# A graph network's gather: a ring of 32 row slots in eight groups in place of 8 slots, and a streamed scale row

## The reference

```python
def gcn_conv(x, W, b, src, dst, n_nodes):      # called twice
    deg  = segment_sum(1, dst) + 1             # with a self loop for every node
    dinv = rsqrt(deg)
    xw   = x @ W
    msg  = xw[src] * (dinv[src] * dinv[dst])
    return segment_sum(msg, dst) + b
out = relu(batch_norm(gcn_conv(layernorm(x), W1, b1, ...)))
out = batch_norm(gcn_conv(out, W2, b2, ...))
x = x + relu(out + layernorm(x))
x = x + moe(layernorm(x))
```

## Time and profile before

| | us |
|---|---|
| the three runs | 7022.28, 7011.63, 6996.64 |
| their median | 7011.63 |
| the profiled execution, span from first to last instruction | 7009.1 |
| aggregation of layer 1, from first to last gather | 295.3 to 2767.7 |
| aggregation of layer 2, from first to last gather | 2908.8 to 5390.0 |

### The profile page before, as it was taken

One profiled execution on the slowest core, in us unless ns is written; L12 is line 12 of the kernel. 1 busy time (PEld: TensorE's weight loads), 2 busy tenths in 40 slices (PEclk: granted clock), 3 DMA queues, 4 the chain that ended last, 5 costly groups with the idle time before them and its releaser, 6 DMA issues. The chain is left out here.

```text
span 7009.1 us, 91724 instructions
## 1 busy us (share of the span) xinstructions
PE 3014.7 (43%) x24826; PEld 1994.5 (28%) x24827; DVE 1748.0 (25%) x6367; ACT 840.1 (12%) x1732; POOL 3732.7 (53%) x3810
## 2 busy tenths in 40 slices
PE   3333333333333334433333333333333443676675
PEld 3222222222222222322222222222222332444443
DVE  9611111111111112511111111111112543222221
ACT  5400000000000000500000000000001542222221
POOL 0266666666666665466666666666664343333333
PEclk5555555555555555555555555555555656888887
DMA  3754444444444443544444444444444343333332
GB/s 90 236 158 133 130 132 133 132 132 132 134 131 132 132 133 109 163 132 134 131 131 132 134 132 133 130 133 130 132 131 114 118 129 106 55 54 53 52 54 45
DMA packets 359556, 847.33 MB, mean 121 GB/s; under 512 B 70751, under 2 KB 183617, under 8 KB 359490
## 3 DMA queue, kind: packets, MB, share of 16 engines
q0 software_dynamic: 254848, 708.96, 38.0%
q1 hardware_dynamic: 104642, 137.62, 6.6%
HBM read 736.62 MB, written 109.69 MB: 121 GB/s over the span
## 5 line engine op out<-in xcount | busy, mean ns | idle before, releaser
L595 POOL DMA_INDIRECT ring<-messages,idx_stage x3328 | 3155.0, 948 | 1944.0 <-PE ps L1579 915.9
L1579 PE MATMUL ps<-onehot_mem,ring 128*128 128x64 bf16 x19968 | 1578.1, 236 | 2874.5 <-DMA ring<-messages,idx_stage 2187.5
L1579 PEld LDWEIGHTS ps<-onehot_mem,ring 128*128 128x128 bf16 x19968 | 1130.9, 123 | 3416.3 <-DMA ring<-messages,idx_stage 2073.1
L1099 DVE TENSOR_TENSOR acc<-acc,ps 128x128 f32 x832 | 240.3, 289 | 3968.9 <-PE ps L1579 2911.3
L650 POOL DMA_INDIRECT out_dram<-acc x216 | 333.4, 1543 | 767.3 <-DMA out_dram<-acc 602.2
L735 ACT ACTIVATE idx_stage<-tables 128x8 int32 (+1 forms) x416 | 86.5, 208 | 4785.8 <-PE ps L1579 3733.8
L1088 DVE TENSOR_SCALAR onehot_mem<-iota_bf,tables 128x64 bf16<-128x64 bf16 x3336 | 600.7, 259 | 105.6 <-issue 81.6
L1612 PE MATMUL ps<-acc,wconv 128*128 (+1 forms) x448 | 346.6, 930 | 245.6 <-DVE rows_mem L1130 194.2
L1807 PE MATMUL ps<-acc 128*128 128x256 f32 x864 | 314.5, 543 | 309.1 <-issue 309.1
L1795 PE MATMUL ps<-acc 128*128 128x512 f32 x864 | 381.7, 595 | 1.3 <-ACT acc L906 1.3
L1807 PEld LDWEIGHTS ps<-acc 128*128 128x128 f32 x864 | 241.7, 287 | 404.6 <-issue 351.6
(11 more groups left out here) (246 smaller groups left out, 2242.2 us busy)
## 6 DMA issues: line engine op xcount, KB each, us to landing
ring<-messages,idx_stage POOLq DMA_INDIRECT x3328
acc<-routed_rows SPq DMA_DIRECT2D x54, 520.0 KB, 3.7
rows_mem<-in_x_dram SPq DMA_DIRECT2D x62, 448.0 KB, 4.2
messages<-dinvT SPq DMA_DIRECT2D x28, 672.0 KB, 5.8
out_dram<-rows_mem SPq DMA_DIRECT2D x28, 448.0 KB
dinvT<-in_x_dram SPq DMA_DIRECT2D x22, 448.0 KB, 4.6
messages<-ring SPq DMA_DIRECT2D x14, 672.0 KB, 3.9
messages<-rows_mem SPq DMA_DIRECT2D x14, 672.0 KB, 3.9
```

The costliest lines, as they stand in the source:

```text
L595: pool.indirect_dma_start(out=slots[:, s, :], out_offset=None, in_=t_dram[layer], in_offset=bass.IndirectOffsetOnAxis(ap=idx_stage[:, u, s ...
L1099: dve.tensor_tensor(sums(w, WIN), sums(w, WIN), partial(u, WIN), ALU.add).then_inc(ev_fast[run], 1)
L1579: last = pe.matmul(ps[:, 2 * u + k, 0:width], slots[:, s, n * D + k * P:n * D + (k + 1) * P], onehot[:, ohu, j, 0:width], start=j == 0 and ...
```

## The change

- `SLOTS` is 32, eight groups of four (`GROUPS`). The slots lie in `dinvT`, and the old `ring` is free for other things.
- GpSimd waits once for each group of four gathers, until the group that had these slots is used; the four gathers of a group share a semaphore (`got[q]`). TensorE waits once a group for all four and counts once a group (`groups_used`, in place of `chunks_used`), with the last of the 24 matmuls. VectorE's, ScalarE's and GpSimd's waits are rewritten to that count.
- ScalarE copies 32 indices at a time.
- TensorE's loop body holds eight groups in place of four; `strides` is told how many groups a call does, and calls it without a loop where only one would be left.
- `dinvT` can't hold the row of inverse root degrees during an aggregation. Each layer streams it in pieces of 448 into `ring` (`dinv_stream`): the last four pieces have a place each (`dinv_tmp[:, 1:]`), the other 24 share one place, and the next is loaded when the one before has been used (`lin_scaled`). Between the layers the whole row is loaded to `dinvT` in one DMA after `agg_done`, and VectorE waits for it before the first `y_cols`.
- Four setup semaphores become two (`all_wanted`, `all_reduced`).

```diff
-SLOTS = 8
+GROUPS = 8
+SLOTS = GROUPS * CPG
...
-        slots = ring_bf.rearrange("p (s f) -> p s f", s=SLOTS)
+        slots = dinvT[:, 0:SLOTS * PARTS * D // 2].bitcast(BF16).rearrange("p (s f) -> p s f", s=SLOTS)
+        LINS = STRIDES - 2
+        dinv_tmp = ring[:, 0:(1 + NCH - LINS) * CH].rearrange("p (u n) -> p u n", n=CH)
...
-            def dinv_load(t):
-                wait(sp, chunks_used, t * DINV_STEP)
-                sp.dma_start(dinvT[:, bass.ds(t * CH, CH)], dinv_row[:, bass.ds(t * CH, CH)].to_broadcast([P, CH])).then_inc(dinv_in, 16)
-
-            dinv_load(0)
-            with sp.Fori(1, NCH) as t:
-                dinv_load(t)
+            def dinv_load(to, t, width=CH):
+                return sp.dma_start(to, dinv_row[:, bass.ds(t * CH, width)].to_broadcast([P, width]))
+
+            def dinv_stream(layer):
+
+                for t in range(LINS, NCH):
+                    dinv_load(dinv_tmp[:, 1 + t - LINS, :], t).then_inc(dinv_last_in, 16)
+                dinv_load(dinv_tmp[:, 0, :], 0).then_inc(dinv_in, 16)
+                with sp.Fori(1, LINS) as t:
+                    sp.wait_ge(lin_scaled[layer], t)
+                    hold(sp)
+                    dinv_load(dinv_tmp[:, 0, :], t).then_inc(dinv_in, 16)
+
+            dinv_stream(L1)
+            sp.wait_ge(agg_done, 1)
+            dinv_load(dinvT[:, 0:NPAD], 0, NPAD).then_inc(dinv_all_in, 16)
...
             in_fours(sp, y_store)
-
+            for q in range(4):
+                sp.wait_ge(stored[q], 16 * (NCH // 4) * 2)
+            dinv_stream(L2)
...
-                def gather(i, u, first):
-                    c0 = i * (2 * SLOTS) + u * SLOTS
-                    pool.wait_ge(stage_ready, i * 2 + u + 1 + done // SLOTS)
-                    for s in range(SLOTS):
-                        wait(pool, chunks_used, c0 + s - SLOTS + 1 + done)
+                def gather(i, u):
+                    n = i * 2 + u
+                    pool.wait_ge(stage_ready, n + 1 + layer * (GATHERS // SLOTS))
+                    for q in range(GROUPS):
+                        wait(pool, groups_used, n * GROUPS + q - GROUPS + 1 + layer * NG)
                         hold(pool)
-                        pool.indirect_dma_start(
-                            out=slots[:, s, :], out_offset=None, in_=t_dram[layer],
-                            in_offset=bass.IndirectOffsetOnAxis(ap=idx_stage[:, u, s:s + 1], axis=0),
-                        ).then_inc(got[s], 16)
+                        for j in range(CPG):
+                            s = q * CPG + j
+                            pool.indirect_dma_start(
+                                out=slots[:, s, :], out_offset=None, in_=t_dram[layer],
+                                in_offset=bass.IndirectOffsetOnAxis(ap=idx_stage[:, u, s:s + 1], axis=0),
+                            ).then_inc(got[q], 16)
...
                 def product_done(n):
 
-                    wait(dve, chunks_used, n * CPG + run * GATHERS if not isinstance(n, int) or n > 0 else 0)
+                    wait(dve, groups_used, n + run * NG if not isinstance(n, int) or n > 0 else 0)
...
                 def scale(t, bank=4):
-                    dve.wait_ge(dinv_in, 16 * NCH)
+                    if isinstance(t, int) and t >= LINS:
+                        dve.wait_ge(dinv_last_in, 16 * (NCH - LINS) * (run + 1))
+                        part = dinv_tmp[:, 1 + t - LINS, :]
+                    else:
+                        dve.wait_ge(dinv_in, 16 * (t + 1 + run * LINS))
+                        part = dinv_tmp[:, 0, :]
...
+            dve.wait_ge(dinv_all_in, 16)
             y_cols(0, 0)
...
                 def fast(i, q):
-                    g, u = i * 4 + q, q % 2
+                    g, u = i * GROUPS + q, q % 2
                     pe.wait_ge(oh_fast[run], g + 1)
                     wait(pe, ev_fast[run], g - 1)
+                    landed(q, i)
                     for j in range(CPG):
-                        s = (q * CPG + j) % SLOTS
-                        landed(s, i * 2 + (q * CPG + j) // SLOTS)
-                        product(u, u, j, s, WIN).then_inc(chunks_used, 1)
+                        last = product(u, u, j, q * CPG + j, WIN)
+                    last.then_inc(groups_used, 1)
```

More of the change, by code:

```diff
@@ L40, in sizes @@
     n_groups = -(-n_edges // GE)
-    stride = -(-n_groups // (4 * n_chunks)) * 4
+    stride = -(-n_groups // (2 * GROUPS * n_chunks)) * 2 * GROUPS
     n_groups += -n_groups % (2 * stride)
@@ L604, in gathers @@
                         for u in range(2):
-                            gather(i, u, False)
+                            gather(i, u)
             gathers(L1)
@@ L727, in aggregate @@
             def aggregate(layer):
-                done = layer * GATHERS
                 def stage(i, u):
-                    wait(act, chunks_used, (i - 1) * (2 * SLOTS) + u * SLOTS + SLOTS + done)
+                    wait(act, groups_used, (i * 2 + u - 1) * GROUPS + layer * NG if not isinstance(i, int) or i + u > 0 or layer else 0)
                     hold(act)
@@ L759, in aggregate @@
                     stages(0)
-                    with act.Fori(1, NG // 4) as i:
+                    with act.Fori(1, NG // (2 * GROUPS)) as i:
                         stages(i)
@@ L1168, in aggregate @@
                     scale(0)
-                    with dve.Fori(1, NCH) as t:
+                    with dve.Fori(1, LINS) as t:
+                        stats(t - 1)
+                        scale(t)
+                    for t in range(LINS, NCH):
                         stats(t - 1)
@@ L1572, in aggregate @@
             def aggregate(run):
-                done = run * GATHERS
                 def product(u, ohu, j, s, width):
@@ L1582, in product, with landed, general @@
                     return last
-                def landed(s, use):
-                    pe.wait_ge(got[s], 16 * (use + done // SLOTS + 1))
+                def landed(q, use):
+                    pe.wait_ge(got[q], 16 * CPG * (use + run * NG // GROUPS + 1))
                 def fast(i, q):
-                    g, u = i * 4 + q, q % 2
+                    g, u = i * GROUPS + q, q % 2
                     pe.wait_ge(oh_fast[run], g + 1)
                     wait(pe, ev_fast[run], g - 1)
+                    landed(q, i)
                     for j in range(CPG):
-                        s = (q * CPG + j) % SLOTS
-                        landed(s, i * 2 + (q * CPG + j) // SLOTS)
-                        product(u, u, j, s, WIN).then_inc(chunks_used, 1)
-                def general(i, u):
-                    g = i * 2 + u
-                    for j in range(CPG):
-                        landed(u * CPG + j, i)
+                        last = product(u, u, j, q * CPG + j, WIN)
+                    last.then_inc(groups_used, 1)
+                def general(i, q):
+                    g = i * GROUPS + q
+                    landed(q, i)
                     hold(pe)
@@ L1628, in lin, with eights @@
                     lin_finish(t)
-                def fours(i):
-                    for q in range(4):
+                def eights(i):
+                    for q in range(GROUPS):
                         fast(i, q)
@@ L1652, in aggregate @@
                 with pe.Else():
-                    with pe.Fori(0, NG // 2) as i:
-                        for u in range(2):
-                            general(i, u)
+                    with pe.Fori(0, NG // GROUPS) as i:
+                        for q in range(GROUPS):
+                            general(i, q)
                     pe.wait_ge(agg_done, run + 1)
```

60 lines of the change are left out of this document (30 added, 30 removed).

## The result

| | us |
|---|---|
| kernel before, 8 executions | 7012.30 median (6996.64 to 7022.28) |
| changed kernel, 8 executions | 7026.99 median (7017.36 to 7035.88) |
| ratio after / before | 1.0026, 95% interval 1.0016 to 1.0036 |
| changed kernel, profiled execution | 7017.36, span 7015.6 |

No gain: 0.26% slower, which is within 0.5% of no change, against a forecast of 6228 us.

What follows compares the result with a forecast made beforehand. GpSimd's gather pace was taken as the floor, with 786.1 us of ring stalls above it. From the span 7009.1: -786.1 + 1.4 + 1.5 = -783.2, so 6225.9; plus 2.5 for the median, 6228 us; range 6195 to 6310.

Steps and rivals of the forecast that it cites:

- I take the whole 786.1 back: Gathers of both aggregations: 32 slots absorb all stalls of GpSimd, -786.1 us (bounds 0 and 786.1); forecast's chance 0.83.
- rival A: Aggregations: every group's release comes 7.4 us late, so the hand-over of used slots sets the pace; +216, 6444 us; chance 0.09.
- C: Aggregations: what makes counts late holds GpSimd as well, so the deeper ring changes nothing; 7010 us; chance 0.03.
- GpSimd's own pace: Gathers of both layers: unstalled starts come 1.253 us apart, so a layer's 1663 intervals would take 2083.7 us.
- D: Gathers: VectorE's one-hots and evictions lock GpSimd out, both layers growing by up to 841, to 7069 us; chance 0.01.
- The last groups of a layer: End of each aggregation: the last group's 24 matmuls come together after its fourth gather; +0.7 a layer, +1.4 in all.
- The whole row before `y_cols`: Between the layers: the 6.42 MB load issued at `agg_done` lands 24.1 us later, against 23.2 us of cover; +1.5 taken.
- The streamed row: Both aggregations: 28 pieces a layer load into the freed `ring` beside the gathers, hidden; uncovered it would cost 192 us.
- One wait a group and the smaller things: Aggregations: fewer GpSimd waits, fewer releases, larger index copies, shared setup semaphores and longer loop bodies change the time by 0.

Runs made afterwards that it cites:

- set 4: Two runs of the changed kernel, edited per layer: SyncE loop, then half rows, 7261.49 us; one gather a group, then 64-row gathers, 5414.81 us; kernel before 7018.77.
- the first set: Changed kernel with four products, eight products, half rows, or one gather a group: 6059.97, 6074.24, 6059.37, 3502.57 us; kernel before 6071.88.
- theory 6: Not a run but an explanation from the follow-ups: the limit is in GpSimd's own gathers, and transfers of another queue cost nothing; no run of its own.

## Why the prediction was wrong

**The step that failed** is "I take the whole 786.1 back": "A late spell of 3 to 10 us is then absorbed, provided that TensorE and VectorE catch up. They can". The term measured +9, not -786.1: the layers take 2480.9 and 2481.8 us from first to last gather (before 2472.4 and 2481.1), with stalls of 400 us in each. The proviso failed. The 48 matmuls in 1.85 us of the earlier trace rows are a burst; the mean pace at which TensorE's counts come is one group in 5.95 to 5.98 us, with 8 slots and with 32, against the 5.01 in which GpSimd can supply one. A deeper buffer evens out a lateness that comes and goes; it gives nothing where the consumer's mean pace is the lower one. With 32 slots the first stall came after gather 36, for a count 37 us late, and then every twelve gathers.

I had the number and used it the wrong way round: against rival A I wrote that "the mean pace is still four chunks in 5.95 us" and took that pace for GpSimd's stalls. It was the consumers' pace that made the stalls. I had also written that I didn't know the cause of the lateness, and still gave 0.83 to a cure that depended on it.

**Which rival came true.** C, "The stalls aren't the ring's", at 7010 us, to which I gave 0.03: the same stalls of some 3 us every dozen gathers, as its sign said. Its words were not quite right, for the cause doesn't hold GpSimd but TensorE and SyncE, and VectorE now and then. My argument against it, that GpSimd's stalled starts end at a release, tells who is waited for and not why that one is late. A, the hand-over as the pace, describes the late counts too, but set 4 speaks against it as their cause: with one gather a group the same hand-over goes in 2.09 us.

**The other terms.**

- GpSimd's own pace, 1.253 us: right, 1.251 in the first set. D was rightly given little: 940, 947, 1297 ns, no gather was held. Whether VectorE's operations here are of the two-port kind, of which the rule beside D speaks, no run shows, so this doesn't test that rule.
- The last groups of a layer, +0.7 each: wrong. From the last gather to the `agg_done` marker are now 15.4 us, before 8.1, and 6.9 us more at the end of layer 2. TensorE is a full ring behind when GpSimd ends (seven evictions follow between 2779.3 and 2789.3, the last gather starts at 2776.45), a cost of a deep ring with a slow consumer: +14.2, not +1.4.
- The whole row before `y_cols`, +1.5: -0.2. The marker is at 2791.86 and the first `y_cols` at 2814.84, 22.98 us where 23.21 were, and ScalarE released it, not the row. The row's load was issued at 2791.95, and its 16 counts are recorded from 2809.61 to 2810.92: 19.0 us, 3.9 us before `y_cols`. So the 24.1 us that I worked out from 291 GB/s were 5 too many, and the load cost nothing. The Trainium skill (DMA: Bandwidth & Descriptors, "Anatomy of one DMA — SWDGE (gpsimd) path") gives by its fit of 2.0 us plus bytes at 436 GB/s an estimate of 16.7 us; its fit is for DMAs that GpSimd issues, this one is SyncE's, and the 19.0 measured lie between the two.
- The streamed row, hidden: right; in the tiles VectorE's scaling starts 0.5 us after the start of the last eviction.
- One wait a group and the smaller things, 0: nothing seen.

Sum: +9.2 for the gathers, +14.2 for the tails, -0.4 between marker and layer 2, +0.3 ahead of layer 1, and behind the tail of layer 2 16.7 us less, where the two kernels do the same work and I have no cause for it; together +6.6, the difference of the spans (7015.6 - 7009.1) but for rounding. The profiled execution is the fastest of its eight; the medians differ by 14.7.

**What holds the engines: shown and open.** Shown: TensorE and SyncE, and VectorE at times, take their instructions in steps of 0.70 us in spells, on some chips only, and far more often in the stretches with four gathers a group than in that with one. The pace is then 1.49 us a gather, whatever its bytes or rows; not bound by TensorE's and VectorE's own work, nor by SyncE's transfers. Not shown: why. One trace of a cause is in the records themselves. Every gather counts its semaphore up 16 times, and its 16 transfers for that are in every trace; of those counts the trace of the changed kernel has 4.6 a gather, that of four products on the faster chip 15.8, and the layer with one gather a group on the slower chip 13.6. So on the slower chips records of counts are missing in just the stretches in which the engines step. A full path for the profiler's records might be behind both the steps and the silence from 342.8 to 346.2 us of the timeline above, in which no engine starts anything, no transfer is under way and the count is still out. That is argued, not shown. Each execution listed here has a span and a clock, so each was recorded, and no run tells what an unrecorded one takes. The Trainium skill (NOTIFIC — the notification-queue block, "7.1 Overflow: three behaviours, one of which stalls the engine") says that the block "always backpressures rather than losing a record inside the block", and that this can throttle an engine; by that rule a full path would hold an engine but lose nothing, so the missing counts would need another reason. No run here shows that path directly, and the weak effect of SyncE's extra instructions speaks against counting records alone. A price for each recorded packet of a transfer is unlikely too: a gather has 64 packets with full rows and 48 with half rows or with 64 rows, and the pace is 1.49 us for all three. It wasn't tried to replace some gathers by other transfers of the same size, which would test theory 6 directly.

## What to carry to other kernels

Before deepening a buffer, compare mean paces: if the consumer's long-run rate equals the stalled producer's, the stalls follow from it, and a deeper ring only moves them and lengthens the tail. A cause that one can't name ("late in spells") is not yet priced; give the rival "something else makes it late" a real chance. When a busy engine idles on "issue", look at an engine that has nothing to do, at the longest of its register instructions and not at their median: where some take 20 times their usual time, something holds the engines that is not the work of either.

## What the hardware did that I had not expected

- The same kernel takes 6053 to 6072 us on some chips and 7012 to 7098 on others, some 16%, with GpSimd's unhindered pace equal (1.25 us a gather).
- Register instructions of SyncE: 33 ns on one chip, in spells some 700 on another; weight loads of TensorE one in 0.70 us with all their data there.
- An indirect gather of 128 rows costs GpSimd 0.947 us at 1,536 B and 0.945 at 768 B a row; one of 64 rows 0.90. Its price is nearly one for the instruction.
- The count of a matmul that by the profile ended at 309.4 is recorded at 346.2.
- One load of 6.42 MB, a row of 50 KB broadcast to 128 partitions, landed 19.0 us after its issue.
